# Merging linear attention with the norm behind it, piping the preparation by 512 tokens, and forming later weights beside the causal attention

## What is computed

```python
mods = silu(c) @ wmod                      # 6 x 128 values per batch and layer
# layer 0, attention: 16 heads of 8, causal, with relu features
q_p, k_p = relu(q @ proj), relu(k @ proj)
out = sum_m q_p * cumsum(k_p * v) / (sum_m q_p * cumsum(k_p) + 1e-6)
# layer 0, feed forward: 64 experts of 32, scores softmaxed, sorted by column, the best groups kept
# layer 1, attention: linear, not causal
q, k = relu(q) + 1e-6, relu(k) + 1e-6
kv = einsum('bnd,bne->bde', k, v)
z = 1 / (einsum('bnd,bd->bn', q, k.sum(1)) + 1e-6)
attn = einsum('bnd,bde,bn->bne', q, kv, z) @ W_out.T + b_out
# layer 1, feed forward: gate, up and down with activations and weights rounded to blockwise FP4
```

## Time and profile before

| | |
|---|---|
| median of 3 runs | 1109.37 us (1109.18 to 1115.99) |
| profiled execution | 1103.91 us, of which span 1102.2 us |
| mean granted TensorE clock | 0.903 |
| PE, DVE, ACT, POOL busy | 864.3, 770.6, 439.3, 125.7 us |

### The profile page before, as it was taken

One profiled execution on the slowest core, in us unless ns is written; L12 is line 12 of the kernel. 1 busy time (PEld: TensorE's weight loads), 2 busy tenths in 40 slices (PEclk: granted clock), 3 DMA queues, 4 the chain that ended last, 5 costly groups with the idle time before them and its releaser, 6 DMA issues. The chain is left out here.

```text
span 1102.2 us, 19778 instructions
## 1 busy us (share of the span) xinstructions
PE 864.3 (78%) x7220; PEld 490.9 (45%) x7220; DVE 770.6 (70%) x1438; ACT 439.3 (40%) x788; POOL 125.7 (11%) x106
## 2 busy tenths in 40 slices
PE   5518999989988775999875847999996986567675
PEld 4216766666665541443322313443443762344443
DVE  1762344688878984999979597888884441778885
ACT  3616566656545431555433750111112247222222
POOL 4420000000000001000000980000000000043330
PEclk8859999999989986999998888999998988678878
DMA  8500000000000000355451538666560000000001
GB/s 187 80 1 2 2 3 2 2 3 2 2 2 2 2 1 1 155 199 193 168 163 68 196 137 250 193 206 209 186 196 0 1 1 1 1 10 10 19 10 29
DMA packets 54054, 79.82 MB, mean 72 GB/s; under 512 B 14352, under 2 KB 28496, under 8 KB 53840
## 3 DMA queue, kind: packets, MB, share of 16 engines
q1 hardware_dynamic: 49584, 76.57, 21.9%
q10 hardware_dynamic: 4384, 2.10, 0.7%
HBM read 40.90 MB, written 35.65 MB: 69 GB/s over the span
## 5 line engine op out<-in xcount | busy, mean ns | idle before, releaser
L1159 PE MATMUL bank<-so_g,Wd 128*128 128x512 f32 x256 | 129.1, 596 | 4.9 <-DVE so_g L1218 4.9
L1398 ACT ACTIVATE so_u<-bank,bu 128x512 f32<-128x512 f32 x128 | 87.5, 685 | 80.3 <-PE bank L57 77.6
L1218 DVE TENSOR_TENSOR so_g<-so_u,bank 128x512 f32<-128x512 f32 x128 | 84.3, 673 | 22.1 <-PE bank L1145 19.0
L903 ACT ACTIVATE att_qk<-bank 128x512 f32<-128x512 f32 x128 | 66.8, 602 | 43.4 <-PE bank L733 43.0
L991 DVE TENSOR_TENSOR att_am<-bank,causal 128x512 f32<-128x512 f32 x64 | 44.0, 688 | 47.5 <-PE bank L767 47.4
L767 PE MATMUL bank<-att_qk 64*128 64x128 f32 x1024 | 76.2, 289 | 0.0
L1499 DVE SCALAR_TENSOR_TENSOR so_made<-bank,bg,so_u 128x512 f32<-128x512 f32 x95 | 68.6, 745 | 7.0 <-DMA hidden<-so_made 5.1
L767 PEld LDWEIGHTS bank<-att_qk 64*128 64x128 f32 x1024 | 63.7, 191 | 20.2 <-issue 20.2
L1159 PEld LDWEIGHTS bank<-so_g,Wd 128*128 128x128 f32 x256 | 47.7, 191 | 54.2 <-issue 32.6
L1383 POOL TENSOR_TENSOR so_made<-so_u,so_g 128x512 f32<-128x512 f32 x33 | 48.1, 1503 | 171.4 <-DVE so_cnt L1554 170.1
L1145 PE MATMUL bank<-F,spread 128*128 (+1 forms) x128 | 47.9, 385 | 18.2 <-DMA F<-so_flo 18.2
(11 more groups left out here) (380 smaller groups left out, 1785.3 us busy)
## 6 DMA issues: line engine op xcount, KB each, us to landing
hidden<-so_made SPq DMA_DIRECT2D x128, 256.0 KB, 2.0
so_u<-hidden SPq DMA_DIRECT2D x64, 512.0 KB, 3.9
xin<-in_L_attn_x_dram ACTq DMA_DIRECT2D x8, 256.0 KB, 8.2
out_dram<-ff_ot SPq DMA_DIRECT2D x8, 256.0 KB, 2.3
so_other<-so_key SPq DMA_DIRECT2D x2, 512.0 KB, 5.6
wm<-in_L_wmod_dram SPq DMA_DIRECT2D x2, 384.0 KB, 5.8
F<-so_fhi SPq DMA_DIRECT2D x4, 128.0 KB, 4.9
F<-so_flo SPq DMA_DIRECT2D x4, 128.0 KB, 4.0
```

The lines of the kernel that those rows point to most:

```text
L903: nc.scalar.activation(qk[t % 2][:, r, :, :].rearrange("p a l -> p (a l)"), psF[r], ACT.Relu).then_inc(s_["fe"], 1)
L1159: nc.tensor.matmul(psY[j][:, :], Wd[:, n, :], hh[n % 4][:], start=False, stop=n == EBLK - 1).then_inc(s_dn[n % 4], 1)
L1218: nc.vector.tensor_tensor(hh[k % 4][:], pg[k // 2 % 4][:, k % 2, :], psW[k % 4][:, :], ALU.mult).then_inc(s_hh[k % 4], 1)
L1398: nc.scalar.activation(u[m % NU_][:], psU[m % 3][:, :], ACT.Silu, bias=bu[:, k:k + 1], scale=1.0 / WS).then_inc(s_u, 1)
```

## The change

**Preparation.** One pipeline over the 8 tiles in place of separate passes. x is transposed as it lands, DVE instead of ACT copies it, and PE goes on at once with `centre` of the tile before and `variance` of the one before that. Silu is made of an exponential, a sum, a reciprocal and a product, so that ACT keeps one table, loaded ahead of the DMA issues. `h_high(u)` waits for the modulation. `Wqkv` and the gates are formed last. `stand()` now covers 30 semaphores; in the kernel before only the norm's 9 were raised ahead of this block.

**Causal attention.** The DMAs of the other weights, the POOL splits (`Wrs`, `bd`, `Wu`) and the FP4 rounding are moved here, into chunks 0 to 12; 13 semaphores are added. `wg_f`, `wu_f`, `wq_n` lie in buffers that are not yet used (`F2f`, `keys`, `RS`).

**Linear attention and ln3.** One block with 6 turns. A turn works on three batches at once: keys, values and queries of batch b; products, division and gate of batch p = b-1, and the norm of its first tile; the norm of the second tile of pp = b-2. Keys and values are evicted by 256 tokens. The output projection is multiplied into `kv` once a batch (`turned`, `projected`), so the projection of each tile and the copy ahead of it are gone. The norm has one bank `psC`, shares `psQ` with the queries, and has one buffer each of `sq`, `rs`, `xn`.

```diff
 # preparation, tensor
-                    ln_pe(pe, 0)
-                    pe.wait_ge(s_lnd, 1)
-                    ln_pe(pe, 1)
+                    upto(pe, "const", N_FIRST)
+                    for u in range(NU):
+                        columns(u)
+                        if u > 0:
+                            centre(u - 1)
+                        if u > 1:
+                            variance(u - 2)
+                        if u == 5:
+                            upto(pe, "silu", 1)
...
 # preparation, scalar
+                    def h_high(u):
+                        b = u // 2
+                        upto(act, "xn", u + 1)
+                        upto(act, "dve", 2)
...
+                    for u in range(NU):
+                        square(u)
+                        if u > 0:
+                            inverse_root(u - 1)
...
+                        if u > 3:
+                            h_high(u - 4)
 # preparation, vector
+                        if u == 6:
+                            upto(dve, "mod", 1)
+                            step(nc.vector.tensor_copy(mod[:].rearrange("p l j b -> p (l j b)"), psMod[:, 0:12 * NB]))
 # causal attention, tensor
+                        def weights(t):
+                            if t == 0:
+                                pe.wait_ge(s_load["w1"], n_load["w1"])
...
+                            if t in (1, 9, 13):
+                                pe.wait_ge(s_["wqd"], FIRST + (1, 9, 13).index(t) + 1)
 # causal attention, vector, at the end of chunk(t)
+                            if t == 2:
+                                dve.wait_ge(s_load["wq"], n_load["wq"])
+                                prepare(fp4_scales(nc, prepare, wq_n, n, work))
+                            if t == 3:
+                                prepare(fp4_divide(nc, wq_n, n, work))
+                            if t == 4:
+                                prepare(fp4_grid(nc, prepare, n, work))
+                            if t == 6:
+                                fp4_scale(nc, prepare, wq_q, n, work).then_inc(s_["wq"], 1)
...
 # linear attention, tensor
-                        with pe.Fori(0, NB) as b:
+                        def centre(t):
+                            upto(pe, "x", t + 1)
+                            upto(pe, "xn", t)
...
+                        def variance(t):
+                            upto(pe, "sq", t + 1)
+                            upto(pe, "ln", t)
...
+                        def turn(b, p, pp):
+                            if b is not None:
+                                keys_values(4 * b)
+                            if p is not None:
+                                turned(p)
+                            if b is not None:
+                                queries(2 * b)
+                                keys_values(4 * b + 1)
+                            if p is not None:
+                                projected(p)
+                            if pp is not None:
+                                centre(2 * pp + 1)
...
+                            if p is not None:
+                                back(2 * p + 1)
+                                centre(2 * p)
+                            if b is not None:
+                                accumulate(4 * b + 3)
+                            if p is not None:
+                                variance(2 * p)
```

## The result

| | before | after |
|---|---|---|
| median of the runs, same chip (4 each) | 1109.28 us (1100.15 to 1115.99) | 1073.68 us (1072.2 to 1077.37) |
| ratio, 95% interval | | 0.9751 (0.9705 to 0.9796) |
| profiled execution, its span | 1103.91, 1102.2 us | 1077.37, 1075.7 us |
| mean granted TensorE clock | 0.903 | 0.907 |

What follows compares the result with a forecast made beforehand. The preparation was taken as a chain of passes, the causal attention as bound by PE. Terms -28.6 + 5 - 14 = -37.6 gave 1066.3 us profiled; with 5.5 us for the median, 1072 us, range 1058 to 1087.

Steps and rivals of the forecast that it cites:

- Preparation, -28.6: Pipelined preparation ends at 46 us against 75.6; causal attention starts at 51.5 instead of 80.1 (bounds -33 to -22).
- ACT's stall: Preparation: `h_high(0)` waits for the modulation, whose 24 products take PE 3.9 us at half clock; ACT stands 3 us.
- ACT ends at 41.5, `Hlo(7)` 0.9 later: End of preparation: ACT sets the pace to 41.5 us, DVE's last low half follows 0.9 later, then `Wqkv` and gates.
- Weights, +5: Weights formed beside the causal attention cost 5 us: transposes, waits in chunks 1, 7, 10, small hops; bounds +1.5 to +16.
- slower: Rival: new waits in the causal attention drop the clock, some 8 us per half-clock chunk; 1125 us, chance 0.02.
- Linear attention with ln3, -14: Merged block walked turn by turn takes 77.7 us, ending at 922.2 instead of 936.2; bounds -22 to -4.
- Turn 4: Merged linear attention and ln3: this turn walked at 13.2 us; called thin, which speaks for a fall of the clock.
- the rival's reason: Merged stage: one-column products with a weight load each don't hold the clock up; two falls, +10, 1082 us, chance 0.14.
- half clock for over 10 us in the merged turns: Sign of a wrong forecast, in the merged linear attention and ln3: PE at half clock for over 10 us.
- The base, +5.5: Whole kernel: median of runs lies 5.5 us above the profiled execution (1109.4 against 1103.9), carried from 1066.3 to 1072 us.

Runs made afterwards that it cites:

- early_tail: Kernel after, with `Wqkv`, the gates and the first full h formed in DVE's idle time between the sixth and eighth tile of the preparation: ratio to before 0.9709.
- after_old_linear: Kernel after, with linear attention in its two old blocks and ln3 as its own stage; new preparation and weights kept: ratio to before 0.9835.
- warm_first: Kernel after, with 6 and 16 idle transposes filling PE's waits for ACT in the causal attention's first chunk: ratio to before 0.9771.
- pool_beside_grid: Kernel after, with GpSimd's splits of bdown and Wup held until the attention's chunk 3 is done, beside DVE's FP4 grid: ratio to before 0.9766.
- last_norm: Kernel after, with second banks and buffers for the last tile's norm, run in turn 4 so that turn 5 is gone: ratio to before 0.9716.
- tail_filler: Kernel after, with 80 idle transposes on PE behind the preparation's last variance, shortening its idle time ahead of the causal attention: ratio to before 0.9745.

## Why the prediction was right in the time and wrong in the gain

**Preparation, -28.6: right, its walk only in part.** The profiles say -27.1 to -30.4. The first product stands at 53.1 us (forecast 51.5), and at 49.8 to 51.0 in six other executions with the same preparation. The block starts at 2.8 and not 3.2 us, and PE at 6.45, not 8.3: the table load did not hold the DMA issues up. ACT's stall was 2.77 us (forecast 3): the 24 products took 2.74 us at full clock. The 3.9 us that I had taken as their price at half clock were mixed, since the clock of before fell to half only at 21.4 us, 1.5 us into them. But ACT, though it set the pace, was neither the busiest engine (21.5 us, DVE 23.3) nor the last. Timeline of the kernel after:

```profile
22.02 2.74 PE L359 MATMUL bank<-prep_cT,prep_wm 128*128 128x4 f32 x24
...
26.40 0.81 ACT L307 ACTIVATE Hhi<-prep_xn,mod 128x512 f16<-128x512 f32 x1 [2.77 <-DVE mod L399]
...
36.52 2.91 ACT L307 ACTIVATE Hhi<-prep_xn,mod 128x512 f16<-128x512 f32 x4
...
42.99 1.29 DVE L388 TENSOR_TENSOR Hlo<-prep_hf,Hhi 128x512 f16<-128x512 f32 x2
...
47.55 0.17 DVE L429 COPY gb_tile<-mod 128x8 f32<-128x8 f32 x1
```

ACT ends at 39.4, 2 us earlier than I had; DVE then still owes `h_full` and `h_low` of the last tiles, 1.06 us a tile, to 44.3, because its first `h_full` stands only behind the sixth tile's normalising. The step "ACT ends at 41.5, `Hlo(7)` 0.9 later" failed: it is 4.9 us later. ACT being early hid it.

**Weights, +5: right.** 4.4 us timed; in the profiles early_tail, which shows neither the fall of the clock in the first chunk nor the halt in chunk 1, takes 1.6 us longer than before to the first `att_cT` and 2.5 us in the twelve chunks. Place by place: chunk 1's scores waited 0.80 us for `Wo` (forecast 1.0), chunk 7's mask cost 1.45 (1.5), chunk 10 0.45 (0.4); chunk 9's 0.75 I did not have apart. The wait for `Wo`, and chunk 7, in the kernel after:

```profile
74.14 0.39 PE L734 MATMUL bank<-above,identb 128*128 128x512 bf16 x1 [0.80 <-DVE Wo L1050]
...
133.84 1.32 DVE L107 TENSOR_TENSOR att_wq_xn<-att_wq_xn,att_sorting 128x1120 f32<-128x1120 f32 x1
135.19 1.32 DVE L108 TENSOR_TENSOR RS<-att_wq_xn,att_wq_sc 128x1120 f32<-128x1120 f32 x1
136.43 0.68 DVE L992 TENSOR_TENSOR att_am<-bank,causal 128x512 f32<-128x512 f32 x1
...
137.22 0.38 PE L734 MATMUL bank<-above,identb 128*128 128x512 bf16 x1 [1.39 <-ACT att_qk L904]
```

The trace puts PE's 1.39 us down to ACT; it is DVE's mask, which ended at 137.11, behind the two scaling operations. A wait for several semaphores names one of them.

**What the sum left out, 5 to 6 us.** The stage grew by 11.4 us in the profiles (345.4 to 356.8) where I had 5. The clock's fall in the first chunk is 3.7 us of the rest, and PE's halt in chunk 1 (below) 1.4, the step's 9.46 us instead of 8.09. Some 2 us lie behind the twelfth chunk, where after_old_linear with the same attention takes no longer than before. The gap behind the stage also grew, from 5.6 to 6.1 us, which I had not counted. The clock's fall was close to the rival "slower", in the attention too, but by a wait that the kernel before has as well, behind an idle time that the change doubled; I had thought only of new waits and of five chunks and more.

**Linear attention with ln3, -14: half to two thirds.** Turns of the kernel after:

```profile
831.15:838.80 7.65, 7.35 (x46) 5.47 (x47) 2.97 (x6) 2.78 (x5) 0.21 (x4) 0.78 0.00 0
838.80:853.40 14.60, 13.15 (x95) 10.36 (x94) 7.21 (x20) 3.71 (x8) 0.00 (x0) 1.00 0.00 1
853.40:870.00 16.60, 15.12 (x99) 11.12 (x98) 8.00 (x19) 8.12 (x15) 0.00 (x0) 1.00 0.00 1
870.00:886.50 16.50, 15.02 (x98) 11.11 (x97) 8.00 (x19) 8.11 (x15) 0.00 (x0) 1.00 0.01 1
886.50:901.70 15.20, 11.48 (x52) 7.09 (x50) 5.13 (x11) 7.05 (x11) 0.00 (x0) 0.89 0.00 0
901.70:911.70 10.00, 4.12 (x4) 1.00 (x4) 1.38 (x2) 4.84 (x7) 0.00 (x0) 0.55 0.00 1
```

I had 8.7, 14.9, 15.9, 15.9, 13.2 and 9.1, 77.7 in all; it is 80.5. The dense turns are within 0.7 us. Turn 4 is the term that was too small, by 2 us: it is thin, and the clock fell to half in it from 889.1 to 892.5 us (0.89), not in the products with one column but ahead of them, behind a wait for ACT:

```profile
888.29 0.49 PE L1733 MATMUL bank<-Wo,la_kvT 128*128 128x128 f32 x2 [1.49 <-ACT la_kvT L1817]
888.96 1.88 PE L1757 MATMUL bank<-XT,centre_w 128*128 128x512 f32 x2 [0.18 <-DVE la_xn L1919]
```

Turns 1 to 3 hold the same products at a clock of 1.00, so the rival's reason, that such products do not hold the clock up, is not borne out here. The sign that I had given for being wrong, half clock for over 10 us in the merged turns, did come, with 15.6 us; but 5.7 and about 9 us of it, in turns 0 and 5, stood in my own walk, so the sign could not tell the two apart. The larger error is in the base: I set the walk against one execution of the old stages with 11.3 us lost to the clock, and the timed runs say 6.5 to 9.3 us. The pairs of profiles, gaps included, say 7.8 (after_old_linear against after) to 11.9 (before against after): both kinds of measurement stay below my 14.

**The base, +5.5.** Carrying the median over the profile was wrong by 7 to 9 us for before on other chips, where the median lies 1.9 to 3.4 us under the profiled execution, and for after the profiled execution lay 3.7 us above its median, not 5.5 below.

## What to carry to other kernels

Work on a chain's end by asking what each engine still owes when the pacing engine is through: here DVE's low halves and gates, which idle time earlier in the same stage could hold, were worth 4.6 us in the time and 2.2 to 5.5 us in the profiles. Small work beside a stage bound by PE costs what its place costs: 2.6 us of DVE in one chunk cost 1.45, in two chunks 0.1. A gain read against a single profiled execution carries that execution's clock with it: compare stages with the time lost to the clock taken off, and expect several us either way in the time.

## What the runs showed of the hardware that I had not expected

**PE stood still in the midst of like matmuls.** Chunk 1 of the kernel after, one row of 16 scores cut in two:

```profile
82.55 0.82 PE L741 MATMUL bank<-att_qk 64*128 64x128 f32 x9
84.37 0.71 PE L741 MATMUL bank<-att_qk 64*128 64x128 f32 x7 [1.00 <-issue]
```

PE waited for nothing that the profile shows. Such a halt of 0.32 to 1.54 us stands between 70 and 85 us in seven of the eleven profiles with the new preparation and in none of the three without. In most the transfers of `Wup` and `Wgate` hold the DMA engines meanwhile (share 1.06 at 83 to 85 us, 294 GB/s), but in warm_first's halt at 70.2 us the share is 0.08, and four profiles with the same transfers show no halt. One may argue that PE's instructions come late: in all seven a transfer of 16 KB on the queue that the page calls instruction ends 1.1 us before the halt to 0.1 us behind its begin, and takes 1.5 to 1.6 us, where others of its size take as little as 0.9 in quieter stretches. The four without a halt have that transfer too, so this is not shown. In pool_beside_grid and last_norm the clock fell behind the halt; in last_norm the twelve chunks lost 1.7 us so.

In pool_beside_grid and tail_filler the clock also fell for some 3 us near chunk 8, where the step takes 9.5 and 9.4 us instead of 8.0; that is a part of their 123.0 and 116.7 us.

**The spread of one kernel goes with the granted clock.** Of 16 runs of before on one chip the fastest was 1096.6 us at a mean of 0.909, the longest 1111.9 at 0.894, and the others lie within some 5 us of the line between.
